# sLSTM stage of a decoder kernel: layers six steps apart in place of seven, and another place for one group of gate products

## Chip, core and metric

The kernel runs on one core of a Trainium2 chip (trn2). The metric is the device time of one execution in microseconds (us). Engines are named as in the profile: PE is TensorE (PEld its weight loads), DVE is VectorE, ACT is ScalarE, POOL is GpSimd, SP is the engine that starts the DMAs of the first stage.

## What is computed

The reference is a decoder block on x of 32 sequences x 256 tokens x 256 features. The change touches only its first part, four sLSTM layers:

```
for l in range(4):
    x = x + slstm_layer(ln(x, ln1[l]), ...)      # recurrence over the 256 tokens
    x = x + ffn(ln(x, ln2[l]), ...)              # gelu(x @ up_g) * (x @ up_v) @ down
return ln(x, post)

slstm_layer(xn):                                  # 4 heads of 64 features
    xc = silu(causal_conv4(xn) + b)               # the convolved rows
    gi, gf = xc @ wi, xc @ wf                     # gate products of the convolved rows
    gz, go = xn @ wz, xn @ wo                     # gate products of the normed rows
    step:  raw = gates + h @ rker + bias          # i, f, z, o
           lfm = m + log_sigmoid(f); mn = max(i, lfm)
           c = exp(lfm-mn)*c + exp(i-mn)*tanh(z); n = exp(lfm-mn)*n + exp(i-mn)
           h = sigmoid(o) * c / n
    out = groupnorm(h)
```

Behind it stand a cross attention and a feed-forward part with quantised weights; they form the second stage, `attend_and_feed`, and the change doesn't touch them.

## The kernel before

**Tiling.** `slstm` runs one loop of `STEPS` steps, written out for each engine. The 128 partitions are four groups of 32: group l holds the 32 sequences of layer l. So each instruction of a step works on all four layers at once, each at its own token. Layer l+1 works `LAG` tokens behind layer l, because a layer's output has to pass the feed-forward part, a DMA to the next group of partitions, the first layer norm, the convolution and the gate products before the next layer can use it. `LEAD` steps lie between the first row's load and layer 0's first recurrent step. With `LAG = 7`, `LEAD = 4` the 256 tokens need `STEPS = 284`.

**One step j on PE, in program order:** transposes of h into bank FD (L249); the last quarter of the up products of the feed-forward part, of step j-1's rows (`feed_up_last`, L309, called at L334); the recurrence, 32 matmuls of h features by recurrent weights (L258, waits for ACT's copy `ht_copied`); `centred`, the group norm's centring (L278); `feed_down` (L285, waits for `grown`); transposes of the normed rows (L249, waits `xn_done`); the bias (L265) and the gate products of the normed rows (`gates_from_normed`, L258); transposes of the after-cell rows xm (waits `xm_done` and `xnt_copied`); the gate products of the convolved rows (`gates_from_convolved`, L258, for step j+1, waits `xs_done`); transposes of the hidden rows (`hidden_features`, L304, waits `hid_done` and `xmt_copied`); the first three quarters of the up products (`feed_up`, L309). All this is one in-order instruction stream; PE carries nothing else in this stage. Products are fp32, and the profile counts two matmuls and two loads for each instruction that isn't a transpose.

**The other engines in a step.** ACT: a table load, exp of `dl` (L369), the copy of the transposed h (`h_features`, L358), two logarithms (L374, L379), rstd (L381), exp and log of gate f (L383, L385), a table load, gelu (L390), the copies `xnt_copied` and `xmt_copied` between tanh of z and d (L358, L394, L396), tanh of o and of the convolution (L399, L401), and the copy of the hidden features. DVE: statistics of h (L493, L496), `grown` (L498), the normaliser, the normed rows, the decay (L513), the cell output, the layer output xo (L524), xm (L526), hidden (L528), the cell update (L532, L536, L539), h (L544), the convolved rows `xst` (L549, `xs_done`; it waits for `gates_in`, since PE reads the old rows), and the statistics of xm and of the next layer inputs. POOL does the convolution's products and sums. SP starts three DMAs: the next input row, the move of the layer outputs to the next groups, and the store of layer 3's output.

**The PSUM banks.** Gates of step j lie in banks 2(j%2) and 2(j%2)+1. The bias starts them, the three groups of products add to them. The transposes of xm and of the hidden rows use the same bank CV, which is why `hidden_features` waits for the copy of xm's transposes.

**Rings.** `xr` has 7 slots for the layer inputs: a row is loaded into slot (j+4)%7, outputs are moved into slot (j+3)%7, its statistics are taken there, the normed rows are made one step later from (j+2)%7, and the residual is read from (j-2)%7. `xnt` has four slots; gates are made from slot (j-2)%4.

Of the kernel before, what the change touches and what calls it, by code (L numbers as in the profile page):

```python
# [17 lines left out]
HEADS = D // DH  # L18
HALF = D // P
GATES = 4  # L20
UT = 112
UTILES = UP // UT

LAG = 7
LEAD = 4
STEPS = 284
FIRST = LEAD + 3 * LAG + 3
XROWS = STEPS + 2
XRING, NRING, MRING, ORING = 7, 4, 4, 4
# [13 lines left out]
ENGINES, DMA = 4, 16  # L43
# [55 lines left out]
def slstm(nc, ctx, a, x4, pieces):  # L99
# [9 lines left out]
    wg = sb("gate_weights", [P, LAYERS, HALF, GATES, DH])  # L109
# [28 lines left out]
    xr = sb("layer_inputs", [P, XRING, D])  # L138
    xo = sb("layer_outputs", [P, ORING, D])
# [13 lines left out]
    stat2, stat1 = sb("bn_stats_ln2", [P, 6]), sb("bn_stats_ln1", [P, 6])  # L153
    mv = sb("mean_var1", [P, HEADS + 2, 2])
    lrs, rs = sb("log_rstd", [P, HEADS + 2]), sb("rstd", [P, HEADS + 2])
    yn = sb("cell_out", [P, D])
    xm = sb("after_cell", [P, MRING, D])
    xn, ct = sb("normed", [P, D]), sb("tanh_half_conv", [P, D])
    gl, hid = sb("gelu_of_gate", [P, UP]), sb("hidden", [P, UP])
    ht = sb("h_features", [P, HALF, P])  # L160
    xst = sb("convolved_features", [P, HALF, P])
    xnt = sb("normed_features", [P, NRING, HALF, P])
# [35 lines left out]
    def by_half(ap, order, halves_first=True):  # L198
        return ap.rearrange(f"p ({'n r d' if halves_first else order}) -> p {order}", r=2, n=HALF)
# [4 lines left out]
    def group(l):  # L204
        return slice(32 * l, 32 * l + 32)
# [4 lines left out]
    with nc.Block() as block:  # L210

        @block.sync
        def _(sy):
            for dst, src in ((wg, a["gate_w"]), (rk, a["rker"]), (up, a["ff_up"]), (down, a["ff_down"]), (conv_w, a["conv_w"]), (conv_b, a["conv_b"]),
                             (ln1, a["ln1"]), (ln2, a["ln2"]), (gnc, a["gn_w"]), (rows, a["bias"])):
                sy.dma_start(dst[:], src).then_inc(w_loaded, DMA)
            sy.wait_ge(zeroed, 1)
            sy.dma_start(xr[group(0), 3, :], a["x"][0]).then_inc(first_x, DMA)
            sy.wait_ge(bias_made, 10)
            sy.dma_start(bias[32:32 + 3 * LAYERS, :], bias[0:3 * LAYERS, :]).then_inc(bias_moved, DMA)  # L220
            sy.dma_start(pick16[32:32 + 3 * LAYERS, :], pick16[0:3 * LAYERS, :]).then_inc(bias_moved, DMA)
            sy.wait_ge(first_x, DMA)

            def row(rows_, j):
                return rows_[j:j + 1].rearrange("o b d -> b (o d)")

            for j in range(STEPS):
                if j > 0:
                    sy.wait_ge(xm_done, j)
                    sy.wait_ge(x_loaded, DMA * j)  # L230
                sy.dma_start(xr[group(0), (j + 4) % XRING, :], row(a["x"], j + 1)).then_inc(x_loaded, DMA)
                sy.wait_ge(xo_done, j + 1)
                if j > 0:
                    sy.wait_ge(x_moved, DMA * j)
                    sy.wait_ge(x_stored, DMA * j)
                sy.dma_start(xr[32:128, (j + 3) % XRING, :], xo[0:96, j % ORING, :]).then_inc(x_moved, DMA)
                sy.dma_start(row(x4, j), xo[96:128, j % ORING, :]).then_inc(x_stored, DMA)
                if 0 <= j - FIRST_PIECE < len(pieces):
                    dst, src, done = pieces[j - FIRST_PIECE]
                    sy.dma_start(dst, src).then_inc(done, DMA)  # L240
            sy.wait_ge(x_loaded, STEPS * DMA)
            sy.wait_ge(x_moved, STEPS * DMA)
            sy.wait_ge(x_stored, STEPS * DMA)

        @block.tensor
        def _(pe):
# [5 lines left out]
            def by_head(j, w, src, g0, g1):  # L252
                for n in range(HALF):
                    for l in range(LAYERS):
                        for odd in range(2):
                            r = slice(DH * odd, DH * odd + DH)
                            at = n * GATES * DH
                            mm = nc.tensor.matmul(bank[group(l), 2 * (j % 2) + odd, at + g0 * DH:at + g1 * DH], src[r, n, group(l)],  # L258
                                                  w[r, l, n, g0:g1, :].rearrange("p g d -> p (g d)"), start=False, stop=True,
                                                  skip_group_check=True)  # L260
                return mm
# [27 lines left out]
            def gates_from_normed(j):  # L289
                pe.wait_ge(ls_done, j + 1)  # L290
                for odd in range(2):
                    add_bias(2 * ((j + 1) % 2) + odd, odd, 512 * odd, 512)
                by_head(j + 1, wg, xnt[:, (j - 2) % NRING], 2, GATES)

            def gates_from_convolved(j):
                if j > 0:
                    pe.wait_ge(xs_done, j)
                by_head(j + 1, wg, xst, 0, 2).then_inc(gates_in, 1)

            def hidden_features(j):  # L300
                pe.wait_ge(hid_done, j + 1)
# [11 lines left out]
            def feed_up_last():  # L313
                feed_up(UPV, UP, 1).then_inc(up_done, 1)
# [14 lines left out]
            for j in range(STEPS):  # L329
                if j > 0:  # L330
                    pe.wait_ge(h_done, 2 * j)
                transposes(FD, D, h, ht_ready)
                if j > 0:
                    feed_up_last()  # L334
                recurrence(j)
                centred(j)
                pe.wait_ge(grown, j + 1)
                if j > 0:
                    pe.wait_ge(hidt_copied, j)
                feed_down(j)  # L340
                pe.wait_ge(xn_done, j + 1)
                transposes(CV, 0, xn, xnt_ready)
                gates_from_normed(j)
                pe.wait_ge(xm_done, j + 1)
                pe.wait_ge(xnt_copied, j + 1)
                transposes(CV, D, xm[:, j % MRING], xmt_ready)
                gates_from_convolved(j)
                hidden_features(j)
                feed_up(UPG, 0, 0)
                feed_up(UPG, 0, 1)  # L350
                feed_up(UPV, UP, 0)
            feed_up_last()
            pe.wait_ge(up_done, STEPS)

        @block.scalar
# [51 lines left out]
        def _(dve):  # L407
# [80 lines left out]
            for j in range(STEPS):  # L488
# [6 lines left out]
                for i in range(HEADS):  # L495
# [5 lines left out]
                nc.vector.scalar_tensor_tensor(out=heads(ls[:]), in0=heads(sp[:]), scalar=never[:, j:j + 1],  # L501
                                               in1=gate(j - 1, 0), op0=ALU.add, op1=ALU.add).then_inc(ls_done, 1)
                dve.wait_ge(rstd_step, 2 * j + 2)
                nc.vector.tensor_scalar(by_half(xn[:], "r n d"), by_half(xr[:, (j + 2) % XRING, :], "r n d", False), mv[:, HEADS + 1, 0:1], rs[:, HEADS + 1:HEADS + 2],  # L504
                                        ALU.subtract, ALU.mult).then_inc(xn_done, 1)
                dve.wait_ge(f_step, 2 * j + 1)
                dve.wait_ge(ls_done, j + 1)
# [37 lines left out]
                                                   scalar=1.0, in1=heads_of(half_r[:], n), op0=ALU.add,  # L545
                                                   op1=ALU.mult).then_inc(h_done, 1)
                dve.wait_ge(ct_done, j + 1)
                dve.wait_ge(gates_in, j + 1)
                nc.vector.scalar_tensor_tensor(out=xst[:].rearrange("p n t -> p (n t)"), in0=ct[:], scalar=1.0, in1=part[:, j % 2, 0],  # L549
                                               op0=ALU.add, op1=ALU.mult).then_inc(xs_done, 1)  # L550
                dve.wait_ge(xm_done, j + 1)
# [3 lines left out]
                dve.wait_ge(x_moved, DMA * (j + 1))  # L555
                if j > 0:
                    dve.wait_ge(x_loaded, DMA * j)
                nc.vector.bn_stats(stat1[:], xr[:, (j + 3) % XRING, :]).then_inc(ln1_stat, 1)
                dve.wait_ge(ln1_stat, j + 1)
                nc.vector.bn_aggr(mv[:, HEADS + 1, :], stat1[:]).then_inc(ln1_mv, 1)  # L560
            dve.wait_ge(xs_done, STEPS)
# [979 lines left out]
```

## Time and profile before

| | |
|---|---|
| device time, median of 3 runs | 4049.7 us (4048.94 to 4052.33) |
| profiled execution | 4048.4 us, its span 4046.7 us |
| first stage | about 47 to 2513 us of the span |
| second stage | from about 2513 us to the end |

The slices of the page (busy share in tenths, 40 slices of the span) show the two stages:

```profile
PE   6999999999999999999999998799999999999997
PEld 3555555555555555555555554466666666666664
DVE  7999999999999999999999998788888888888886
ACT  4999999999999999999999998466666666666665
POOL 3666666666666666666666666444344443444443
PEclk9999999999999999999999999899999999999998
```

In the first stage PE, DVE and ACT are all busy for over nine tenths, so the busy shares alone don't tell which of them sets the length of a step. For that the order of the instructions within a step is read from the timeline. A step repeats with almost no variation, so one step stands for all.

### The profile page before, as it was taken

To read this page: it belongs to the slowest core of one execution; us is meant where nothing else is said; L and a number is where in the kernel's file an instruction comes from. 1 tells how busy PE (TensorE), PEld (TensorE's weight loads), DVE (VectorE), ACT (ScalarE), POOL (GpSimd) and SP (SyncE) were. 2 spreads that over 40 slices of the span, in tenths; PEclk is the share of its full clock that TensorE was granted. 3 is DMA by queue.
4 is the path that set the end of the run, shared out by engine and by line. 5 is a ranking of instruction groups with operands and counts; after the bars stand their busy time and mean duration, and the time that the engine had idled before them with its cause. 6 is when DMAs were issued, how large, how long until landed. Compare 5 with 4: busy or idle time off the path is not lost. (4 is left out here: it accounts for less than half of the span.)

```text
span 4046.7 us, 170045 instructions
## 1 busy us (share of the span) xinstructions
PE 3876.7 (96%) x70778; PEld 2189.0 (54%) x70778; DVE 3681.0 (91%) x10771; ACT 3256.1 (80%) x6720; POOL 2211.6 (55%) x2425
## 2 busy tenths in 40 slices
PE   6999999999999999999999998799999999999997
PEld 3555555555555555555555554466666666666664
DVE  7999999999999999999999998788888888888886
ACT  4999999999999999999999998466666666666665
POOL 3666666666666666666666666444344443444443
PEclk9999999999999999999999999899999999999998
DMA  2000111000000000000000000000000001000000
GB/s 77 21 23 23 48 54 51 21 23 23 21 23 23 21 23 23 21 23 23 21 23 23 21 23 24 17 22 23 31 24 23 23 22 33 23 22 22 26 21 9
DMA packets 101034, 105.27 MB, mean 26 GB/s; under 512 B 17536, under 2 KB 96032, under 8 KB 99768
## 3 DMA queue, kind: packets, MB, share of 16 engines
q1 hardware_dynamic: 100264, 94.39, 8.0%
q8 instruction: 558, 9.14, 1.0%
q14 instruction: 212, 1.74, 0.1%
HBM read 48.68 MB, written 17.69 MB: 16 GB/s over the span
## 5 line engine op out<-in xcount | busy, mean ns | idle before, releaser
L596 POOL TENSOR_TENSOR conv_products<-normed_features,conv_taps_by_token 128x256 f32<-128x256 f32 (+1 forms) x852 | 780.4, 916 | 609.7 <-DVE convolved_features L549 358.5
L309 PE MATMUL banks<-up_centred,after_cell_features 128*32 128x336 f32 x9088 | 759.6, 452 | 0.0
L786 POOL TENSOR_TENSOR exps_of_both_halves<-scores 128x256 f32<-128x256 f32 x512 | 419.1, 842 | 619.9 <-ACT scores L1042 614.7
L285 PE MATMUL banks<-down,hidden_features 112*32 112x256 f32 x6816 | 427.5, 384 | 0.0
L365 ACT ACT_TABLE_LOAD x284 | 364.4, 1283 | 52.7 <-PE banks L265 47.8
L586 POOL TENSOR_TENSOR conv_partial_sums<-conv_products,conv_partial_sums 128x512 f32<-128x512 f32 x284 | 364.8, 1285 | 66.6 <-DVEq L485 44.4
L1042 ACT ACTIVATE scores<-scores 128x512 f32<-128x512 f32 x512 | 305.4, 626 | 116.3 <-DVE scores L1190 115.4
L309 PEld LDWEIGHTS banks<-up_centred,after_cell_features 128*32 128x32 f32 x9088 | 237.2, 109 | 270.6 <-issue 270.6
L386 ACT ACT_TABLE_LOAD x284 | 364.4, 1283 | 5.0
L1190 DVE SCALAR_TENSOR_TENSOR scores<-banks,score_top 128x512 f32<-128x512 f32 x512 | 327.7, 681 | 27.0 <-PE banks L872 26.4
L258 PE MATMUL banks<-recurrent_weights,h_features 64*32 64x256 f32 x9088 | 311.7, 383 | 1.4 <-ACT h_features L358 1.4
L882 PE MATMUL banks<-scores,v_tokens 128*32 128x256 f32 x4096 | 273.9, 385 | 27.4 <-ACT scores L1042 26.6
L588 POOL TENSOR_TENSOR conv_partial_sums<-conv_products,conv_partial_sums 128x256 f32<-128x256 f32 x284 | 209.0, 736 | 145.9 <-DVE normed L504 145.9
L590 POOL TENSOR_TENSOR conv_partial_sums<-conv_products,conv_partial_sums 128x256 f32<-128x256 f32 x284 | 206.6, 728 | 127.8 <-DVE minus_decay_logit L513 127.8
L285 PEld LDWEIGHTS banks<-down,hidden_features 112*32 112x32 f32 x6816 | 192.7, 109 | 124.1 <-issue 1.1
L258 PEld LDWEIGHTS banks<-recurrent_weights,h_features 64*32 64x32 f32 x9088 | 138.9, 106 | 191.8 <-ACT h_features L358 156.1
L532 DVE SCALAR_TENSOR_TENSOR banks<-half_cell_ratio,tanh_z 128x256 f32<-128x256 f32 x284 | 223.2, 786 | 0.0
L850 PE MATMUL banks<-batch_inputs_hi,qkv_weights_hi 128*128 128x256 f16 x1024 | 196.3, 273 | 10.0 <-POOL batch_inputs_lo L774 8.5
L850 PE MATMUL banks<-batch_inputs_lo,qkv_weights_hi 128*128 128x256 f16 x1024 | 196.2, 273 | 0.0
L850 PE MATMUL banks<-batch_inputs_hi,qkv_weights_lo 128*128 128x256 f16 x1024 | 196.2, 273 | 0.0
L258 PE MATMUL banks<-gate_weights,convolved_features 64*32 64x128 f32 x9088 | 189.5, 275 | 0.0
L258 PE MATMUL banks<-gate_weights,normed_features 64*32 64x128 f32 x9088 | 189.5, 275 | 0.0
(215 smaller groups left out, 10055.6 us busy)
## 6 DMA issues: line engine op xcount, KB each, us to landing
layer_inputs<-layer_outputs SPq DMA_DIRECT2D x284, 96.0 KB, 2.0
layer_inputs<-in_x SPq DMA_DIRECT2D x285, 32.0 KB, 1.8
x_scratch<-layer_outputs SPq DMA_DIRECT2D x284, 32.0 KB, 1.8
x_tokens<-in_x SPq DMA_DIRECT2D x32, 256.0 KB, 3.1
context_features<-in_ctx SPq DMA_DIRECT2D x32, 256.0 KB, 3.8
layers_out<-x_scratch SPq DMA_DIRECT2D x32, 256.0 KB, 2.9
out<-result SPq DMA_DIRECT2D x64, 128.0 KB, 1.8
up_centred<-in_ff_up SPq DMA_DIRECT2D x1, 2688.0 KB
```

Source lines behind the costliest of these rows:

```text
L258: mm = nc.tensor.matmul(bank[group(l), 2 * (j % 2) + odd, at + g0 * DH:at + g1 * DH], src[r, n, group(l)], w[r, l, n, g0:g1, :].rearrange( ...
L285: mm = nc.tensor.matmul(bank[group(l), FD, 0:D], hidt[:, i, group(l)], down[:, l, i, :], start=i == 0, stop=i == UTILES - 1, skip_group_ch ...
L309: mm = nc.tensor.matmul(bank[group(l), b, 0:UP], xmt[:, n, group(l)], up[:, l, n, at:at + UP], start=n == 0, stop=n == HALF - 1, skip_grou ...
L365: nc.scalar.preload_act_table_set(LOG_EXP)
L386: nc.scalar.preload_act_table(ACT.Gelu)
L586: nc.gpsimd.tensor_tensor(new[:, 0:2], prod[:, 0:2], old[:, 1:3], ALU.add).then_inc(conv_done, 1)
L596: nc.gpsimd.tensor_tensor(prod[:, i:i + n], xnt[:, j % NRING].rearrange("p n t -> p (n t)")[:, None, :].broadcast_to([P, n, HALF * P]), ta ...
L786: nc.gpsimd.tensor_tensor(psum[:, i % RING, :], pr[:, i % RING, 0:S], pr[:, i % RING, S:2 * S], ALU.add).then_inc(halves_added, 1)
L850: mm = nc.tensor.matmul(bank[:, b, i * S:(i + 1) * S], w_[:, m, h, (2 * n + i) * P:(2 * n + i + 1) * P], x_[:, j % SLOTS, src, h, :], star ...
L882: mm = nc.tensor.matmul(bank[32 * g:32 * g + 32, b, at:at + S], stationary(kt, i), pr[:, i % RING, kt * S:(kt + 1) * S], start=kt == 0, st ...
L1042: nc.scalar.activation(pr[:, i % RING, :], pr[:, i % RING, :], ACT.Exp, scale=S_SCALE).then_inc(exp_done, 1)
L1190: nc.vector.scalar_tensor_tensor(out=pr[:, i % RING, :].rearrange("p (k s) -> p k s", k=KT), in0=bank[:, i % SCORES, :].rearrange("p (k s) ...
```

## The change

`LAG` goes from 7 to 6, `LEAD` from 4 to 3 and `STEPS` from 284 to 280. `gates_from_convolved` now makes the products for the same step instead of the next one, and moves from behind the transposes of xm to behind the transposes of h. The last quarter of the up products, which stood there, moves to the end of its own step, right behind the other three. Slots of `xr` and `xnt` move by one. DVE's write of the convolved rows waits for one completion of `gates_in` fewer.

```diff
-LAG = 7
-LEAD = 4
-STEPS = 284
+LAG = 6
+LEAD = 3
+STEPS = 280
...
-            sy.dma_start(xr[group(0), 3, :], a["x"][0]).then_inc(first_x, DMA)
+            sy.dma_start(xr[group(0), LEAD - 1, :], a["x"][0]).then_inc(first_x, DMA)
...
-                sy.dma_start(xr[group(0), (j + 4) % XRING, :], row(a["x"], j + 1)).then_inc(x_loaded, DMA)
+                sy.dma_start(xr[group(0), (j + LEAD) % XRING, :], row(a["x"], j + 1)).then_inc(x_loaded, DMA)
...
-                sy.dma_start(xr[32:128, (j + 3) % XRING, :], xo[0:96, j % ORING, :]).then_inc(x_moved, DMA)
+                sy.dma_start(xr[32:128, (j + 2) % XRING, :], xo[0:96, j % ORING, :]).then_inc(x_moved, DMA)
...
-                by_head(j + 1, wg, xnt[:, (j - 2) % NRING], 2, GATES)
+                by_head(j + 1, wg, xnt[:, (j - 1) % NRING], 2, GATES)
 
             def gates_from_convolved(j):
-                if j > 0:
-                    pe.wait_ge(xs_done, j)
-                by_head(j + 1, wg, xst, 0, 2).then_inc(gates_in, 1)
+                pe.wait_ge(xs_done, j)
+                by_head(j, wg, xst, 0, 2).then_inc(gates_in, 1)
...
                 transposes(FD, D, h, ht_ready)
                 if j > 0:
-                    feed_up_last()
+                    gates_from_convolved(j)
                 recurrence(j)
...
                 transposes(CV, D, xm[:, j % MRING], xmt_ready)
-                gates_from_convolved(j)
                 hidden_features(j)
                 feed_up(UPG, 0, 0)
                 feed_up(UPG, 0, 1)
                 feed_up(UPV, UP, 0)
-            feed_up_last()
+                feed_up_last()
...
                 dve.wait_ge(ct_done, j + 1)
-                dve.wait_ge(gates_in, j + 1)
+                if j > 0:
+                    dve.wait_ge(gates_in, j)
```

On DVE the normed rows come from slot (j+1)%7 and the statistics of the next layer inputs from (j+2)%7.

## Rows read from the trace of the kernel before

**Rows 1.** The page: span, and busy time (share) of each engine.
```profile
span 4046.7 us, 170045 instructions
PE 3876.7 (96%) x70778; PEld 2189.0 (54%) x70778; DVE 3681.0 (91%) x10771; ACT 3256.1 (80%) x6720; POOL 2211.6 (55%) x2425
```
**Rows 2.** Stretches: length, busy us (PE, PEld, DVE, ACT, POOL), PEclk, DMA share, GB/s.
```profile
0.00:60.00 60.00, 23.28 (x233) 12.65 (x233) 41.19 (x114) 9.89 (x20) 7.04 (x16) 0.89 0.33 114
...
1000.00:1100.00 100.00, 98.31 (x2246) 50.68 (x2248) 95.10 (x321) 91.51 (x198) 63.09 (x70) 1.00 0.09 23
```
**Rows 3.** Copy of transposed h, 60 to 2480: durations (ns), first and last start.
```profile
L358 ACT ACTIVATE h_features<-banks x279: 384/384/387, 68.2 to 2478.0; 128x256 f32<-128x256 f32 x140
```
**Rows 4.** Timeline, PE in one step: start us, us, engine, line, tiles.
```profile
1005.25 1.09 PE L258 MATMUL banks<-recurrent_weights,h_features 64*32 64x256 f32 x32
...
1009.55 0.20 PEld L249 LDWEIGHTS banks<-identity,after_cell 128*128 128x128 f32 x2 [0.38 <-DVE after_cell L526]
1009.92 0.67 PE L258 MATMUL banks<-gate_weights,convolved_features 64*32 64x128 f32 x32
1010.53 0.30 PEld L304 LDWEIGHTS banks<-identity,hidden 128*112 128x112 f32 x3 [0.21 <-issue]
1011.00 1.90 PE L309 MATMUL banks<-up_centred,after_cell_features 128*32 128x336 f32 x24
1012.83 0.20 PEld L249 LDWEIGHTS banks<-identity,h 128*128 128x128 f32 x2 [0.55 <-issue]
1013.20 0.77 PE L309 MATMUL banks<-up_centred,after_cell_features 128*32 128x336 f32 x8
1013.90 1.09 PE L258 MATMUL banks<-recurrent_weights,h_features 64*32 64x256 f32 x32
```
**Rows 5.** Timeline of the same step, ACT.
```profile
1006.45 0.38 ACT L383 ACTIVATE softplus_logs<-banks 128x256 f32<-128x256 f32 x1
...
1009.06 0.38 ACT L358 ACTIVATE normed_features<-banks 128x256 f32<-128x256 f32 x1
1010.03 0.39 ACT L358 ACTIVATE after_cell_features<-banks 128x256 f32<-128x256 f32 x1
1013.31 0.38 ACT L358 ACTIVATE h_features<-banks 128x256 f32<-128x256 f32 x1
1014.55 0.30 ACT L379 ACTIVATE log_rstd<-mean_var,eps 128x6 f32<-128x6 f32 x1 [0.38 <-DVE mean_var L496]
1015.10 0.38 ACT L383 ACTIVATE softplus_logs<-banks 128x256 f32<-128x256 f32 x1
```
**Rows 6.** Timeline of the same step, DVE.
```profile
1009.21 0.56 DVE L528 SCALAR_TENSOR_TENSOR hidden<-banks,rstd,gelu_of_gate 128x336 f32<-128x336 f32 x1
1011.69 0.49 DVE L544 SCALAR_TENSOR_TENSOR h<-tanh_half_o,half_cell_ratio 128x128 f32<-128x128 f32 x2
1012.10 0.42 DVE L549 SCALAR_TENSOR_TENSOR convolved_features<-tanh_half_conv,conv_partial_sums 128x256 f32<-128x256 f32 x1
```
**Rows 7.** Timeline: DVE loses 0.46 us; what PE and ACT do a step later.
```profile
586.23 0.43 DVE L536 SCALAR_TENSOR_TENSOR banks<-tanh_half_d,banks 128x256 f32<-128x256 f32 x1 [0.46 <-DVE banks L532]
...
598.09 0.61 PEld L258 LDWEIGHTS banks<-recurrent_weights,h_features 64*32 64x32 f32 x32 [0.55 <-ACT h_features L358]
599.29 0.39 ACT L383 ACTIVATE softplus_logs<-banks 128x256 f32<-128x256 f32 x1 [0.37 <-PE banks L258]
602.39 0.20 PEld L249 LDWEIGHTS banks<-identity,after_cell 128*128 128x128 f32 x2 [0.38 <-DVE after_cell L526]
```
**Rows 8.** Timeline, up products of the loop's last step: four quarters in one run.
```profile
2510.37 2.47 PE L309 MATMUL banks<-up_centred,after_cell_features 128*32 128x336 f32 x32
```
**Rows 9.** Timeline, the loop's first step and the start of the second.
```profile
47.69 0.69 PE L249 MATMUL banks<-identity,h 128*128 128x128 f32 x2
49.82 1.96 PE L258 MATMUL banks<-recurrent_weights,h_features 64*32 64x256 f32 x32 [1.45 <-ACT h_features L358]
59.07 0.44 PE L249 MATMUL banks<-identity,h 128*128 128x128 f32 x2
```

More of the change, by code:

```diff
@@ L503, in _ @@
                 dve.wait_ge(rstd_step, 2 * j + 2)
-                nc.vector.tensor_scalar(by_half(xn[:], "r n d"), by_half(xr[:, (j + 2) % XRING, :], "r n d", False), mv[:, HEADS + 1, 0:1], rs[:, HEADS + 1:HEADS + 2],
+                nc.vector.tensor_scalar(by_half(xn[:], "r n d"), by_half(xr[:, (j + 1) % XRING, :], "r n d", False), mv[:, HEADS + 1, 0:1], rs[:, HEADS + 1:HEADS + 2],
                                         ALU.subtract, ALU.mult).then_inc(xn_done, 1)
@@ L557, in _ @@
                     dve.wait_ge(x_loaded, DMA * j)
-                nc.vector.bn_stats(stat1[:], xr[:, (j + 3) % XRING, :]).then_inc(ln1_stat, 1)
+                nc.vector.bn_stats(stat1[:], xr[:, (j + 2) % XRING, :]).then_inc(ln1_stat, 1)
                 dve.wait_ge(ln1_stat, j + 1)
```

## The prediction

> **What bounds the kernel now.** I read the page first, for the shares of the whole span [rows 1], then the busy times of a stretch of the first stage, then the timeline of one step, engine by engine. The page can't name the bound: PE 96%, DVE 91%, ACT 80%. In a stretch of the first stage they are 98, 95 and 92 of 100 us, at the full granted clock, 1.00 of 2.4 GHz [rows 2]. Three engines so close to full mean a ring of work through all of them, and the order has to be walked.
>
> The length of a step: the copy of the transposed h ran 279 times with 278 steps between its first start at 68.2 and its last at 2478.0, so (2478.0 - 68.2) / 278 = 8.668 us [rows 3]. A single undisturbed step takes 13.90 - 5.25 = 8.65 us from recurrence to recurrence [rows 4]; the difference is a few disturbed steps.
>
> Call r the start of the recurrence (1005.25) and walk on from it. ACT's exp of gate f starts at 1006.45, r+1.20 [rows 4, 5]. Does it wait for PE, or merely come after ACT's own work? In the plain step one can't see it, but one disturbed step tells: there ACT sat idle for 0.37 us, was released by PE, and started at 599.29, with the recurrence at 598.09: again r+1.20 [rows 7]. So the recurrence sets it. From there ACT runs without a gap over the log of f, a table load, gelu and the copy of the normed features, which ends at 1009.44 (1009.06 + 0.38) [rows 5]; PE transposes xm 0.11 us later, at 1009.55, r+4.30 [rows 4]. In the disturbed step this is again 602.39 - 598.09 = 4.30 [rows 7]. ACT's copy of that ends at 1010.42 (1010.03 + 0.39) [rows 5]. In between PE does the gate products of the convolved rows, and at 1010.53, r+5.28, the transposes of the hidden rows; the up products follow at 1011.00, the transposes of h at 1012.83, r+7.58, the last quarter of the up products, and the next recurrence at 1013.90, r+8.65 [rows 4]. That is one ring: recurrence, ACT, transposes of xm, then PE alone. Its length is the step.
>
> A second ring is as long. DVE goes from the hidden rows at 1009.21 [rows 6] without a pause to the statistics of h, which release ACT's log of the variance at 1014.55 after 0.38 us of idling; exp of f comes at 1015.10, 8.65 after the last [rows 5]. So a longer PE ring costs at once, and a shorter one would gain nothing.
>
> **The change part by part.**
>
> *Four steps fewer.* 4 x 8.668 = 34.7 us less. The first step, from 47.69 to 59.07, is longer [rows 9] and stays.
>
> *The convolved products leave their place.* They filled 1010.53 - 1009.92 = 0.61 us between the two transposes [rows 4]. What could move up? The transposes of the hidden rows wait for the hidden rows, done at 1009.77 [rows 6], and for ACT's copy of xm's transposes, done at 1010.42 [rows 5]. The handoff from a copy to PE took 0.11 us at the transposes of xm (1009.44 to 1009.55). That gives 1010.53, exactly where they start now. So nothing moves up: the products were free there, they covered the wait for the copy, and PE now stands idle for about 0.6 us in each step. Behind the waiting instruction, in PE's queue, stand all four quarters of the up products and the transposes of h, so the whole tail of the step starts no earlier. Term: 0.00.
>
> *The last quarter of the up products joins the other three.* Alone it took 1013.90 - 1013.20 = 0.70 us. In one run it costs less: the kernel's last step already has this order, and its run of four took 2.47 us against 1.90 for three [rows 8, 4]. Term: +0.57, the transposes of h go from r+7.58 to r+8.15. Are they then limited by something else? h is done at 1012.18, r+6.93 [rows 6]: no.
>
> *The convolved products stand between the transposes of h and the recurrence.* They take 0.61 us at their old place, and the transposes before them 0.37 (1012.83 to 1013.20) [rows 4], together 0.98. But the recurrence also waits for ACT's copy of h: that ended at 1013.69, 0.86 after the transposes started [rows 5], plus the handoff of 0.11 is 0.97. Both say 0.97, in place of 1.07 now (1012.83 to 1013.90). Term: -0.10. Should the products be shorter ahead of the recurrence than ahead of transposes, the copy keeps the 0.97 all the same. The added wait for the convolved rows is free: DVE ends them at 1012.52, r+7.27 [rows 6], and PE asks for them at r+8.15+0.37 = r+8.52, 1.25 us later. Behind this wait the recurrence is queued, and ACT for it, so it would cost in full if it came late. DVE's own wait for `gates_in` gets easier, since the products that read the old rows are now done at the start of the step and not near its end.
>
> *Bias, normed products, DMAs, slots.* The same instructions at the same distance from what they need: outputs are moved and their statistics taken in the same step as before, rows are loaded one step ahead as before, the normed features were copied a step earlier. SP and POOL are passed by nothing. Term: 0.
>
> *Sum.* 0.00 + 0.57 - 0.10 = +0.47 us for a step; 8.668 becomes 9.14. Over 280 steps 280 x 0.47 = +131.6 us, less 34.7 is +96.9. On the profiled execution of 4048.4 us (span 4046.7) that gives 4145.3; the median of the runs lies 1.3 above it: 4146.6. I take 4145, the third digit of a step being rounding (0.01 us in each step is 2.8 us).
>
> *Bounds.* Upwards: the handoff before the recurrence could stay at the 1.07 of now, +0.10, and a transpose's matmul after a wait could cost 0.03 more than one that follows other work; 0.13 x 280 = +36. Downwards: two handoffs of 0.11 and the copy's start 0.48 after its transposes are read from one step each; if the shift left 0.08 of them unneeded, -22. So 4123 to 4181 on the terms alone.
>
> **The rivals.**
>
> *The PE ring is not the bound; faster.* If the DVE ring alone set the step and the exp of f only followed ACT's own work, a longer PE stream would be hidden, and only the four steps would show: 4049.7 - 34.7 = 4015. It decides from one point: PE's ring must grow by less than 34.7 / 280 = 0.124 us. For it speaks that PE's weight loads are busy for only 50.7 of 100 us and DVE for 95.1 [rows 2]. The Trainium skill reads such a profile this way: Perfetto Trace Analysis, section Identifying the Most-Contended Engine, says to judge TensorE by its weight loads and not by its matmul time, and calls the engine of the highest occupancy the contended one, here DVE. By that reading the result is 4015. Against it speaks the disturbed step, in which ACT sat idle with PE as its releaser, and the sum of PE's ring, which comes out at 8.65 without a gap apart from ACT's part [rows 4, 5, 7]. Chance 6%.
>
> *The granted clock falls; slower still.* With an idle 0.6 us in each step, PE could be granted 1.2 GHz at times. The stretch before 60 us, with the loop's first step in it, has a mean granted clock of 0.89 of 2.4 GHz, below the 1.00 of the steady loop [rows 2], so part of it ran at the lower level. What that costs is seen in that step: the recurrence took 1.96 us against 1.09, and the step 59.07 - 47.69 = 11.38 against 8.67 [rows 9, 4]. If one step in ten were of that kind, 28 x 2.7 = 76 us come on top: about 4221. Against it: the stretch read is at 1.00 throughout, with PE idle in every step before the transposes of xm. The Trainium skill, TensorE: Matmul & The Clock Gate, section A second HAM failure mode: psum-queue depth-cycling, has a kernel whose short idle stretches between groups of matmuls make the clock swing between its levels; by that rule this rival would hold, and no row of this case shows it in the steady loop. Chance 3%.
>
> *The convolved rows come late.* A DMA or DVE's tail would have to lose 1.25 us in each step; DVE has 0.47 us more room in the longer step, not less. Each 0.1 us beyond that point is 28 us. Chance 2%. That the change doesn't shorten the loop can be excluded, since the steps are a constant.
>
> *Something covers part of the hole*, so that the two terms cancel the four steps nearly: within 0.2%, 4042 to 4058. It takes a growth of 0.1 to 0.15 us; no row gives such a value. Chance 2%.
>
> **How the numbers follow.** Forecast 87%, the faster rival 6%, no change 2%, clock 3%, late rows 2%. The range takes the bounds above, tightened at the top since both paths before the recurrence gave 0.97: 4118 to 4176; outside it lie the rivals' 13% and a few per cent of the forecast's own. A run of this kernel can be told from no change from about 0.2% (8 us). Faster by more than that: 0.06; within: 0.02; slower: 0.92.
>
> **What would show it.** In the changed kernel's timeline the transposes of the hidden rows should be released by ACT's copy of the after-cell features, 0.11 us after its end, with PE idle for about 0.6 us between the two transposes; the up products should be one run of 32 matmuls of about 2.47 us; recurrence to transposes of h 8.15, on to the next recurrence 0.97; a step of 9.12 to 9.14. ACT should no longer wait for the mean and variance of h but for the recurrence (about 0.5 us), and DVE should show idle time of about the same size. The prediction is wrong if a step stays at 8.67, if the hidden transposes start before r+5.28, or if the clock row of the first stage falls below 1.00.

## The result, and the profile after

The changed kernel takes 4125.59 us (median of 4 runs, 4124.55 to 4126.27) against 4049.32 us of the kernel before on the same chip: ratio 1.0187, 95% interval 1.0169 to 1.0205. It is 76 us slower; forecast were 95 us more, 4145.

The page, the stretch that answers to the one of [rows 2], and the copy of the transposed h that answers to [rows 3] (the stretches give length, busy us of PE, PEld, DVE, ACT and POOL, then PEclk):

```profile
span 4124.5 us, 168128 instructions
PE 3798.7 (92%) x69966; PEld 2202.2 (53%) x69966; DVE 3688.4 (89%) x10659; ACT 3209.7 (78%) x6652; POOL 2184.4 (53%) x2401
```

```profile
60.00:2400.00 2340.00, 2156.12 (x50328) 1162.75 (x50334) 2163.43 (x7227) 2022.51 (x4387) 1412.81 (x1550) 1.00 0.10 25
1000.00:1100.00 100.00, 92.09 (x2147) 49.76 (x2148) 92.41 (x310) 86.50 (x189) 60.36 (x67) 1.00 0.08 22
```

```profile
L356 ACT ACTIVATE h_features<-banks x267: 384/384/387, 60.2 to 2472.4; 128x256 f32<-128x256 f32 x134
```

No engine is near full any more: PE has gone from 98 to 92 us in 100, DVE from 95 to 92, ACT from 92 to 87. A step now takes (2472.4 - 60.2) / 266 = 9.068 us against 8.668, 0.400 more. 280 x 9.068 less 284 x 8.668 is 77 us, which is the whole difference of the spans (4124.5 - 4046.7 = 77.8). The second stage has nothing to do with it.

One step of PE, of ACT and of DVE (one line) in the timeline, which answers to [rows 4, 5, 6]:

```profile
1003.88 1.10 PE L258 MATMUL banks<-recurrent_weights,h_features 64*32 64x256 f32 x32
...
1008.22 0.41 PE L249 MATMUL banks<-identity,after_cell 128*128 128x128 f32 x2
1009.16 0.29 PEld L303 LDWEIGHTS banks<-identity,hidden 128*112 128x112 f32 x3 [0.78 <-DVE hidden L526]
1009.19 0.51 PE L303 MATMUL banks<-identity,hidden 128*112 128x128 f32 x3 [0.57 <-ACT after_cell_features L356]
1009.63 2.47 PE L308 MATMUL banks<-up_centred,after_cell_features 128*32 128x336 f32 x32
1012.03 0.44 PE L249 MATMUL banks<-identity,h 128*128 128x128 f32 x2
1012.40 0.67 PE L258 MATMUL banks<-gate_weights,convolved_features 64*32 64x128 f32 x32
1012.95 1.10 PE L258 MATMUL banks<-recurrent_weights,h_features 64*32 64x256 f32 x32
```

```profile
1005.08 0.38 ACT L381 ACTIVATE softplus_logs<-banks 128x256 f32<-128x256 f32 x1 [0.31 <-PE banks L258]
...
1008.23 0.43 ACT L394 ACTIVATE tanh_half_d<-minus_decay_logit 128x256 f32<-128x256 f32 x1
1008.66 0.39 ACT L356 ACTIVATE after_cell_features<-banks 128x256 f32<-128x256 f32 x1
...
1012.51 0.39 ACT L356 ACTIVATE h_features<-banks 128x256 f32<-128x256 f32 x1 [0.55 <-PE banks L249]
```

```profile
1004.34 0.42 DVE L496 SCALAR_TENSOR_TENSOR growth<-banks,minus_decay_logit 128x256 f32<-128x256 f32 x1 [0.25 <-ACT banks L372]
```

With r at 1003.88 the ring reads: exp of f at r+1.20, now openly waiting for PE; transposes of xm at about r+4.3; then PE idle for 0.57 us, released by ACT's copy, and the transposes of the hidden rows at r+5.31 (their matmul; the load of the weights is 0.03 earlier, r+5.28); the up products in one run of 2.47 us; transposes of h at r+8.15; the recurrence 0.92 us after them, at r+9.07. Every mark of PE is where it was forecast but the last, which was put at 0.97. The idle time is shared out otherwise than told: ACT waits 0.31 us for the recurrence, where about 0.5 was forecast, and 0.55 us more for the transposes of h, where it had no gap before; DVE has one gap of 0.25 us, half of what was forecast.

### The profile page after: what moved, and what is told of

Read it like the earlier page. It is cut to its first block and busy times, and to the rows that moved or that the text cites. A ratio compares the mean times of both kernels' runs of the same rounds, so it can differ in the third digit from the quotient of the medians.

```text
span 4124.5 us, 168128 instructions
## 1 busy us (share of the span) xinstructions
PE 3798.7 (92%) x69966; PEld 2202.2 (53%) x69966; DVE 3688.4 (89%) x10659; ACT 3209.7 (78%) x6652; POOL 2184.4 (53%) x2401
## 5 line engine op out<-in xcount | busy, mean ns | idle before, releaser
L595 POOL TENSOR_TENSOR conv_products<-normed_features,conv_taps_by_token 128x256 f32<-128x256 f32 (+1 forms) x840 | 765.0, 911 | 603.6 <-DVE convolved_features L548 354.5
L308 PE MATMUL banks<-up_centred,after_cell_features 128*32 128x336 f32 x8960 | 691.0, 449 | 0.0
L308 PEld LDWEIGHTS banks<-up_centred,after_cell_features 128*32 128x32 f32 x8960 | 262.5, 109 | 305.4 <-issue 305.4
L303 PE MATMUL banks<-identity,hidden 128*112 128x128 f32 x840 | 143.3, 279 | 158.2 <-ACT after_cell_features L356 158.2
L356 ACT ACTIVATE h_features<-banks 128x256 f32<-128x256 f32 x280 | 107.8, 385 | 152.6 <-PE banks L249 152.6
L303 PEld LDWEIGHTS banks<-identity,hidden 128*112 128x112 f32 x840 | 82.7, 134 | 216.7 <-DVE hidden L526 215.9
```

The costliest lines, as they stand in the source:

```text
L308: mm = nc.tensor.matmul(bank[group(l), b, 0:UP], xmt[:, n, group(l)], up[:, l, n, at:at + UP], start=n == 0, stop=n == HALF - 1, skip_grou ...
L595: nc.gpsimd.tensor_tensor(prod[:, i:i + n], xnt[:, j % NRING].rearrange("p n t -> p (n t)")[:, None, :].broadcast_to([P, n, HALF * P]), ta ...
```

## Experiments

Each kernel was timed beside the kernel before, on the same chip. The length of a step is, as in [rows 3], the span from the first to the last copy of h divided by the steps between.

### The last quarter's new place alone

```diff
                 transposes(FD, D, h, ht_ready)
-                if j > 0:
-                    feed_up_last()
                 recurrence(j)
...
                 feed_up(UPV, UP, 0)
-            feed_up_last()
+                feed_up_last()
```

> The kernel before (LAG 7, 284 steps) with one edit: the last quarter of the up products stands at the end of its own step, the gate products of the convolved rows stay where they are. Nothing stands between the transposes of h and the recurrence any more. My theory (the quarter's new place is the whole cost, the products' old place was free): transposes of h at r+8.15 in place of r+7.58, then the copy of h sets the recurrence, 0.92 to 0.97 later, so a step of 9.07 to 9.12 us in place of 8.668, 114 to 128 us in all: 4163 to 4178 us. Rival theory (the cost of the change is that the convolved products leave a hole and are then paid for again, 0.55 to 0.6 us a step): here they have not moved, so the step stays near 8.65 and the time near 4049.

Measured: 4161.04 us (ratio 1.0278, 1.026 to 1.0296), 2 us below the range of my theory and far from the rival's 4049. The step takes (2471.4 - 60.2) / 266 = 9.065 us. Timeline of PE's weight loads, and of ACT:

```profile
1002.61 0.20 PEld L249 LDWEIGHTS banks<-identity,h 128*128 128x128 f32 x2 [0.55 <-issue]
1003.52 0.62 PEld L258 LDWEIGHTS banks<-recurrent_weights,h_features 64*32 64x32 f32 x32 [0.71 <-ACT h_features L356]
```

```profile
1003.09 0.38 ACT L356 ACTIVATE h_features<-banks 128x256 f32<-128x256 f32 x1 [0.55 <-PE banks L249]
```

This kernel has no idle stretch before the hidden transposes, its convolved products are where they were, and its step is as long as that of the changed kernel. So the products' hole costs nothing, and the whole growth of the step comes from the up products' last quarter. The recurrence follows the transposes of h by 0.91 us although nothing stands between: ACT's copy sets it, and the handoff from its end (1003.47) takes 0.05 us. So at its old place, beside that copy, the quarter cost 1.07 - 0.91 = 0.16 us of the ring; at its new one it costs 0.57.

### The changed kernel without the convolved products

```diff
             def gates_from_convolved(j):
                 pe.wait_ge(xs_done, j)
-                by_head(j, wg, xst, 0, 2).then_inc(gates_in, 1)
...
                 dve.wait_ge(ct_done, j + 1)
-                if j > 0:
-                    dve.wait_ge(gates_in, j)
```

The second part belongs to the first: without the products nothing counts `gates_in` up, so DVE can't wait for it.

> The changed kernel with the gate products of the convolved rows left out (32 matmuls a step; gates i and f lack that part). My theory: between the transposes of h and the recurrence they lie beside ACT's copy of h, which ends 0.87 us after the transposes start and hands over in 0.05 us or more, so the recurrence still starts at 0.92 and the step stays 9.06: 4124 us, within 4. Rival theory (they are paid for by their own length, 0.55 us): the step falls to the other ring's 8.65, 116 us less: about 4010.

Measured: 4146.07 us (ratio 1.0241, 1.0225 to 1.0257): 32 matmuls a step less, and 20 us slower than with them. Neither theory had that.

```profile
1002.23 0.65 PEld L258 LDWEIGHTS banks<-recurrent_weights,h_features 64*32 64x32 f32 x32 [0.77 <-issue]
```

```profile
1001.74 0.38 ACT L356 ACTIVATE h_features<-banks 128x256 f32<-128x256 f32 x1 [0.55 <-PE banks L249]
```

The copy ends at 1002.12 and the load follows 0.11 us later, the matmul 0.14. In the run above it was 0.05. What differs on PE is the wait on `xs_done`: with the products gone it stands, long satisfied, directly ahead of the wait for the copy. That this wait is the reason is a guess so far; the next kernel tests it.

### One satisfied wait more

```diff
             def recurrence(j):
+                if j > 0:
+                    pe.wait_ge(h_done, 2 * j)
                 pe.wait_ge(ht_copied, j + 1)
```

> The changed kernel with one more wait ahead of the recurrence, on h of this step, which has been satisfied for about 2.7 us by then. Theory 1 (a handoff to PE takes about 0.05 us when the instruction has one wait, and 0.11 to 0.14 when a second wait stands ahead of it, whether satisfied or not): the recurrence moves from 0.92 to about 1.00 us behind the transposes of h, 0.07 to 0.08 us a step, 20 to 22 us: 4146 us, as in the run without the convolved products. Theory 2 (the handoff in that run was long because PE had nothing to do in between; a satisfied wait is free): 4125, within 3.

Measured: 4149.31 us (ratio 1.0244, 1.023 to 1.0258), 24 us above the changed kernel.

```profile
1001.00 0.40 PEld L258 LDWEIGHTS banks<-gate_weights,convolved_features 64*32 64x32 f32 x32 [0.17 <-issue]
1001.61 0.65 PEld L258 LDWEIGHTS banks<-recurrent_weights,h_features 64*32 64x32 f32 x32 [0.21 <-issue]
```

```profile
1001.11 0.38 ACT L358 ACTIVATE h_features<-banks 128x256 f32<-128x256 f32 x1 [0.55 <-PE banks L249]
```

The copy ends at 1001.49, the load comes 0.12 later. Over all steps between 60 and 2400 us the median from the copy's end to the load is 0.114 us here and in the kernel without the products, 0.051 in the changed kernel and in the one with only the quarter moved; it scatters by about 0.001. A second wait ahead of an instruction costs 0.07 to 0.08 us in a step although it has been satisfied for some 2 us: theory 1. In every case seen the two waits are for two different engines; two waits for one engine were not tried. The Trainium skill, Perfetto Trace Analysis, section Identifying Dependency Chains, says that an instruction that waits for several engines may have a separate semaphore instruction put ahead of it. The measured handoffs fit that, but the profile doesn't show such an instruction.

### One wait fewer at the hidden transposes

```diff
             def hidden_features(j):
-                pe.wait_ge(hid_done, j + 1)
                 pe.wait_ge(xmt_copied, j + 1)
...
+                act.wait_ge(hid_done, j + 1)
                 act.wait_ge(xmt_ready, j + 1)
                 copy(both(xmt[:]), bank[:, CV, D:], xmt_copied)
```

> The changed kernel with one wait fewer ahead of the transposes of the hidden rows: ACT's copy of the after-cell features waits for the hidden rows in PE's place (they are ready 0.26 us before it starts), PE waits for that copy alone. Theory 1 (number of waits sets the handoff): hidden transposes 0.06 to 0.09 us earlier in the ring, r+5.20 in place of r+5.28, 17 to 25 us in all: 4100 to 4108 us. Theory 2: 4125, within 3.

Measured: 4126.1 us (ratio 1.0185, 1.0171 to 1.0199): no change.

```profile
1007.09 0.43 ACT L393 ACTIVATE tanh_half_d<-minus_decay_logit 128x256 f32<-128x256 f32 x1
1007.59 0.38 ACT L355 ACTIVATE after_cell_features<-banks 128x256 f32<-128x256 f32 x1
```

```profile
1008.02 0.29 PEld L302 LDWEIGHTS banks<-identity,hidden 128*112 128x112 f32 x3 [0.77 <-ACT after_cell_features L355]
```

PE's handoff did fall, from 0.11 to 0.05 (1007.97 to 1008.02). But ACT's copy now starts 0.50 us after the tanh ahead of it, and in the changed kernel it was 0.43 (1008.23 to 1008.66). The second wait has the same price on ACT, and the ring passes through both. The expectation failed because it priced the wait on one engine only.

### The last quarter back between the transposes of h and the recurrence

```diff
                 transposes(FD, D, h, ht_ready)
                 if j > 0:
+                    feed_up_last()
                     gates_from_convolved(j)
...
                 feed_up(UPV, UP, 0)
-                feed_up_last()
+            feed_up_last()             # once, behind the loop
```

> The changed kernel with the last quarter of the up products back between the transposes of h and the recurrence, ahead of the convolved products. My theory (a sum along PE's ring): hidden transposes at r+5.28, transposes of h at r+7.58, then 0.37 + 0.70 + 0.55, recurrence at r+9.20: 0.13 to 0.14 us a step longer than the changed kernel, 4162 us, 4155 to 4170. Rival theory (the quarter's place is what costs, as in the kernel before it is nearly free there): back near 8.65 a step, 4010 to 4020.

Measured: 4132.46 us (ratio 1.0207, 1.0191 to 1.0223): 7 us above the changed kernel, where 36 were expected.

```profile
1004.19 0.44 PE L249 MATMUL banks<-identity,h 128*128 128x128 f32 x2
1004.56 0.77 PE L308 MATMUL banks<-up_centred,after_cell_features 128*32 128x336 f32 x8
1005.26 0.67 PE L258 MATMUL banks<-gate_weights,convolved_features 64*32 64x128 f32 x32
1005.73 1.12 PE L258 MATMUL banks<-recurrent_weights,h_features 64*32 64x256 f32 x32
...
1010.00 0.20 PEld L249 LDWEIGHTS banks<-identity,after_cell 128*128 128x128 f32 x2 [0.38 <-DVE after_cell L525]
```

The products take 0.47 us here (1005.26 to 1005.73), where the copy of h is long done and they really hold up the recurrence; the expectation had 0.55, and ahead of transposes they took 0.61 [rows 4]. That is 0.08 of a miss of about 0.11 us a step; the rest, some 0.03 us, lies between the recurrence and the transposes of xm (10.00 - 5.73 = 4.27 where it was 4.30). Here PE's sum counts in full and the changed kernel is the better of the two by a little, since its products lie beside ACT's copy.

### Layers seven steps apart again

```diff
-LAG = 6
+LAG = 7
-STEPS = 280
+STEPS = 283
...
-                sy.dma_start(xr[32:128, (j + 2) % XRING, :], xo[0:96, j % ORING, :]).then_inc(x_moved, DMA)
+                sy.dma_start(xr[32:128, (j + 3) % XRING, :], xo[0:96, j % ORING, :]).then_inc(x_moved, DMA)
```

> The changed kernel with layers seven steps apart again (inputs are moved one slot later, 283 steps), the order of PE untouched. My theory: the distance of the layers acts through the number of steps alone, the step stays 9.07: 3 x 9.07 = 27 us more, 4153 us. Rival theory (the shorter distance itself lengthens the step, through inputs or convolved rows that come late): the step falls below 9.0 and the time below 4125.

Measured: 4151.9 us (ratio 1.0254, 1.0238 to 1.027), 26 us above the changed kernel for three steps more, and a step of (2471.0 - 68.5) / 265 = 9.066 us. The shorter distance works as told: it takes steps away and does nothing to their length.

### The hole filled

```diff
                 transposes(CV, D, xm[:, j % MRING], xmt_ready)
+                products_of_normed(j)      # taken out of gates_from_normed; the bias stays there
                 hidden_features(j)
```

> The changed kernel with the gate products of the normed rows moved into PE's idle stretch between the transposes of the after-cell rows and those of the hidden rows. My theory: work ahead of the transposes of the after-cell rows is off the ring, as these wait for ACT; the hole moves to before them (about 0.75 us), the hidden transposes stay at r+5.28 (4.30 + 0.34 + 0.61 is 5.25), the step stays 9.07: 4125 us, within 4. Rival theory (idle time of PE is what costs, so filling it pays): 0.55 us a step less as far as the other ring allows, 8.65: about 4010.

Measured: 4126.73 us (ratio 1.0187, 1.0173 to 1.0201): no change.

```profile
1002.60 0.62 PEld L258 LDWEIGHTS banks<-recurrent_weights,h_features 64*32 64x32 f32 x32
...
1006.91 0.20 PEld L249 LDWEIGHTS banks<-identity,after_cell 128*128 128x128 f32 x2 [1.00 <-DVE after_cell L527]
1007.27 0.40 PEld L258 LDWEIGHTS banks<-gate_weights,normed_features 64*32 64x32 f32 x32 [0.17 <-issue]
1007.88 0.29 PEld L305 LDWEIGHTS banks<-identity,hidden 128*112 128x112 f32 x3 [0.21 <-issue]
```

The hidden transposes stand at r+5.28 as before, now behind products; the idle time has moved ahead of the transposes of xm, where 1.00 us passes between two loads in place of 0.38. An idle stretch of PE on this part of the ring is room, and no cost.

### The room used: repacked

The same as the last kernel, and in the room ahead of the transposes of xm the last quarter of the up products:

```diff
                 gates_from_normed(j)
+                pe.wait_ge(yn_done, j + 1)
+                if j > 0:
+                    feed_up_last()
                 pe.wait_ge(xm_done, j + 1)
...
-                feed_up(UPG, 0, 1)
+                feed_up(UPG, 0, 1).then_inc(upg_done, 1)
                 feed_up(UPV, UP, 0)
-                feed_up_last()
+            feed_up_last()             # once, behind the loop
...
-                    act.wait_ge(up_done, j)
+                    act.wait_ge(upg_done, j)
...
+                dve.wait_ge(xm_done, j + 1)
+                nc.vector.bn_stats(stat2[:], xm[:, j % MRING]).then_inc(ln2_stat, 1)
                 dve.wait_ge(gelu_done, j + 1)
+                if j > 0:
+                    dve.wait_ge(up_done, j)
...
-                dve.wait_ge(xm_done, j + 1)
-                nc.vector.bn_stats(stat2[:], xm[:, j % MRING]).then_inc(ln2_stat, 1)
```

Left out here: the centring now adds to cleared banks (`start=False`).

> As the kernel with the normed products in the hole, and in the stretch that this frees the last quarter of the up products, ahead of the transposes of the after-cell rows (PE then waits for the cell output, gelu waits only for the gate half of the up products, DVE for the value half, and DVE takes the statistics of the after-cell rows before the hidden rows, so that the later quarter delays nothing). Centring adds to cleared banks in place of clearing them. My theory: PE's ring shrinks to 5.28 + 0.47 + 1.84 + 0.92 = 8.51 us, so the ring through DVE sets the step, 8.65 to 8.67; with 280 steps 34 us under the kernel before: 4015 us, 4008 to 4030. If this stays near the changed kernel's 4125, the quarter's place is not the cost.

Measured: 3973.34 us (ratio 0.9809, 0.9795 to 0.9822), the fastest kernel of this study: 77 us under the kernel before, 152 under the changed one.

```profile
1000.00:1100.00 100.00, 99.49 (x2301) 51.67 (x2300) 93.69 (x332) 92.59 (x202) 64.33 (x71) 1.00 0.09 23
```

```profile
L363 ACT ACTIVATE h_features<-banks x278: 383/383/388, 67.8 to 2426.0; 128x256 f32<-128x256 f32 x139
```

A step is (2426.0 - 67.8) / 277 = 8.513 us, PE's sum to the hundredth, and PE is busy for 99.5 of 100 us. The expected 4015 was too high by 42 us: DVE's ring, which was to hold the step at 8.65, was shorter than that. This kernel holds several edits at once; the next two kernels show which of them shortened DVE's ring.

### What DVE's ring is worth

Two kernels ask for it. One puts DVE's statistics back in the repacked kernel:

```diff
-                dve.wait_ge(xm_done, j + 1)
-                nc.vector.bn_stats(stat2[:], xm[:, j % MRING]).then_inc(ln2_stat, 1)
                 dve.wait_ge(gelu_done, j + 1)
```

> The repacked kernel with DVE's statistics of the after-cell rows back at their old place, behind the convolved rows. DVE then idles for about 0.35 us ahead of the hidden rows, as the last quarter of the up products ends later than before. Theory A (DVE's ring is as long as the prediction said, 8.65 us, and the repacked kernel is shorter only because its first product of the cell update no longer meets POOL's product, 0.42 us in place of 0.79): 8.65 + 0.37 - 0.36 = 8.66, 4014 us. Theory B (DVE's ring had room all along and only PE's sum counts): the step stays 8.51, 3973 us.

The other makes the opposite edit, and nothing else, in the kernel before:

> The kernel before with one edit on DVE: statistics of the after-cell rows ahead of the hidden rows. Both theories have PE's ring at 8.65 there, so the time stays 4049, within 4. What the trace is to show: if the meeting with POOL's product is what stretches the cell update's first product, it falls from 787 to about 430 ns, as it now starts when POOL's product is nearly done, and ACT no longer waits for the mean and variance of h for 0.38 us (theory A: about 0.36 us less); theory B: the product keeps its 787 ns.

Measured: 4004.77 us (ratio 0.9893, 0.9878 to 0.9908) for the first, step (2453.1 - 68.1) / 276 = 8.641; 4046.64 us (ratio 0.9994, 0.9985 to 1.0004) for the second.

The cell update's first product between 60 and 2400 us in the kernel before, in that second kernel and in the first (durations in ns, least, median, most), and, last line, what the first kernel's hidden rows wait for:

```profile
L532 DVE SCALAR_TENSOR_TENSOR banks<-half_cell_ratio,tanh_z x270: 433/787/796, 64.6 to 2396.4; 128x256 f32<-128x256 f32 x135
```

```profile
L534 DVE SCALAR_TENSOR_TENSOR banks<-half_cell_ratio,tanh_z x270: 423/424/684, 65.5 to 2395.8; 128x256 f32<-128x256 f32 x135
```

```profile
L539 DVE SCALAR_TENSOR_TENSOR banks<-half_cell_ratio,tanh_z x271: 421/459/793, 64.8 to 2397.9; 128x256 f32<-128x256 f32 x136
DVE hidden L535 <- PE banks L311: 83.9, 269, 0.7
```

What POOL and DVE do around it in the kernel before, then in the kernel with the statistics first, then in the repacked kernel with the statistics back:

```profile
1009.51 0.73 POOL L596 TENSOR_TENSOR conv_products<-normed_features,conv_taps_by_token 128x256 f32<-128x256 f32 x1 [0.51 <-ACT normed_features L358]
1009.75 0.78 DVE L532 SCALAR_TENSOR_TENSOR banks<-half_cell_ratio,tanh_z 128x256 f32<-128x256 f32 x1
```

```profile
1006.12 0.39 ACT L383 ACTIVATE softplus_logs<-banks 128x256 f32<-128x256 f32 x1 [0.46 <-PE banks L258]
...
1009.19 0.73 POOL L596 TENSOR_TENSOR conv_products<-normed_features,conv_taps_by_token 128x256 f32<-128x256 f32 x1 [0.51 <-ACT normed_features L358]
...
1009.81 0.42 DVE L534 SCALAR_TENSOR_TENSOR banks<-half_cell_ratio,tanh_z 128x256 f32<-128x256 f32 x1
```

```profile
1007.11 0.73 POOL L604 TENSOR_TENSOR conv_products<-normed_features,conv_taps_by_token 128x256 f32<-128x256 f32 x1 [0.52 <-ACT normed_features L363]
...
1007.58 0.55 DVE L539 SCALAR_TENSOR_TENSOR banks<-half_cell_ratio,tanh_z 128x256 f32<-128x256 f32 x1
```

In the kernel before POOL works from 1009.51 to 1010.24, DVE's product starts in the midst of that and takes 0.78 us. With the statistics ahead it starts 0.11 us before POOL ends and takes 0.42. ACT then waits for PE for 0.46 us and no more for the mean and variance (4 times in 270 steps, 266 times before), and the time is the same, since PE's ring is still 8.65. So DVE's ring did stand at 8.65 in the kernel before, as long as PE's, but 0.36 us of it was this meeting. The first kernel's 4004.8 lies 9 us under the 4014 of theory A and 31 above theory B: DVE's place for the statistics matters, and the step is again set by DVE, at 8.64. That it came out 0.02 lower than theory A's 8.66 fits the rows: DVE waits 0.31 us for PE ahead of the hidden rows (84 us in 269 times) where 0.37 had been assumed, and the product, still partly stretched, has a median of 0.46 us. 8.65 + 0.31 - (0.79 - 0.46) = 8.63, and 8.64 was measured.

## Why the prediction came out as it did

The forecast was right in direction and mechanism; the size was 95 us where 76 were measured, inside the range.

*The ring and its bound: right.* The disturbed step was the decisive row: it showed that exp of f waits for PE at r+1.20, and the changed kernel shows the same r+1.20 with ACT idle in every step.

*The convolved products' old place, 0.00: right.* The hidden transposes stayed at r+5.28, and the kernel that moves only the quarter has the same step without any hole.

*The quarter, +0.57: right,* r+8.15, and shown alone (4161 us).

*Transposes of h to the recurrence, -0.10: too small.* Measured 0.92 in place of 1.07, -0.15. The step that failed is the handoff: 0.11 us was read at the transposes of xm, which have two waits, and used for the recurrence, which has one. With one wait it is 0.05. The products beside the copy were mis-sized too, 0.61 us where they take 0.47 ahead of the recurrence, but, as the prediction allowed for, the copy alone then sets the recurrence. 0.97 - 0.92 = 0.05 us, times 280, is 14 us of the 19. The bound put on that term, 1.07, lay on the wrong side; the lower side was given 0.08 for two handoffs and held it.

*The base.* The terms were taken from the plain step, 8.65, and added to the mean step, 8.668. The mean of the changed kernel lies 0.00 above its plain step (9.068 against 9.07, which is read to 0.01), where it lay 0.018 above before: with room on DVE and ACT a disturbed instruction delays nobody. That is the rest, 0.018 x 280 = 5 us. That the room is the reason is argued, not shown.

*The distance of the layers, 34.7 us for four steps: right in kind.* It was measured at the new length: 26 us for three steps.

*Rivals.* The reading by which DVE, the busiest engine by occupancy against PE's weight loads, would decide and give 4015 fell: the changed kernel has more idle time on DVE and is 76 us slower. The rule of Perfetto Trace Analysis in the Trainium skill has the engine judged by an average, and here the order of the step decided: the repacked kernel ran with weight loads busy for 52 of 100 us and with the length of PE's sum. The rival of a falling clock was priced too high: of the 2.7 us that the first step is longer, 1.06 lie between the transposes of h and the recurrence (49.82 - 47.69 = 2.13 against 1.07), where PE sat waiting for ACT's copy [rows 9], so the clock has 1.67 us of it at most. The rival fell as well: 1.00 from 60 to 2400 us with an idle 0.57 us in each step, so the section of the Trainium skill on short idle stretches (TensorE: Matmul & The Clock Gate, A second HAM failure mode: psum-queue depth-cycling) doesn't describe this kernel. The convolved rows weren't late: PE shows no wait for them, and the products follow the transposes of h by 0.37 us (1012.03 to 1012.40), as the quarter did before.

*The second ring.* The prediction said it was as long and left it there. For its own question that was enough, for the version that was looked for later it wasn't: the 8.65 of that ring held 0.36 us of a meeting with POOL which an order of DVE's own work takes away.

## What to carry to other kernels

Walk the ring of the step before moving work: a group of matmuls that stands where its engine waits for another is free, and the same group in the part where PE alone carries the ring costs all the time it takes there (0.57 us for the quarter); the busy shares don't tell these places apart. Where two rings are equally long, one step in which some engine was disturbed lays open a wait that the plain step hides. When work moves into the PE-only part, look at once for room elsewhere in the step to put something else there: with the shorter distance kept and the last quarter in such room, the kernel went from 4126 to 3973 us.

## What the runs showed of the hardware

- **A second wait costs although it is satisfied.** A handoff from ACT to PE took 0.051 us with one wait ahead of the instruction and 0.114 us with two (medians over the steps of a run); on ACT a copy with two waits started 0.07 us later than with one. The two waits were for two different engines each time.
- **What a group of matmuls costs depends on what follows.** The same 32 matmuls of the convolved rows took 0.61 us ahead of transposes and 0.47 us ahead of the recurrence. In the kernel with the last quarter back the recurrence's weight loads start at 1005.62, 0.11 us before its first matmul; ahead of transposes no load starts more than 0.03 us early:

```profile
1005.62 0.75 PEld L258 LDWEIGHTS banks<-recurrent_weights,h_features 64*32 64x32 f32 x32
```

- **DVE and POOL hold each other up.** A DVE product of two tensors in SBUF took 0.79 us when it started early in a product of POOL and 0.42 us when it hardly met it. The rows above say more: where it started 0.24 or 0.47 us after POOL's product, it ended 0.29 us after that product in both cases (1010.53 after 1010.24, 1008.13 after 1007.84), as if it got going only when POOL was through. In two steps of the kernel before DVE's product and POOL's started within 3 ns of each other; there DVE's took its 0.43 us, and POOL's took 1.01 and 1.02 us in place of 0.73. A second place in each step shows the same, the sum xm, whose two sources are in SBUF: it takes 0.50 us and ends 0.28 us after POOL's sum; in the one step in which POOL didn't meet it, the first, it took 0.42.

```profile
1008.27 0.73 POOL L590 TENSOR_TENSOR conv_partial_sums<-conv_products,conv_partial_sums 128x256 f32<-128x256 f32 x1 [0.46 <-DVE minus_decay_logit L513]
1008.78 0.50 DVE L526 TENSOR_TENSOR after_cell<-cell_out,layer_inputs 128x256 f32<-128x256 f32 x1
```

The Trainium skill, GPSIMD Engine Reference, section 1. Specifications, says that POOL shares SBUF interfaces with VectorE and names DVE instructions with two SBUF inputs; the rows agree.
